# Evened code masks, a filtered sequence in other buffers, and earlier splits in a vision tower on one core

## The reference

```python
h = 2 * Re(einsum(x * (A - 1) / log A, A ** t))         # t = 0..1023: (32, 64, 1024)
h = h + attention(layernorm(h)) @ Wo                    # 16 heads of 64, rotary, causal
h = h + layernorm(h) @ (NF4_CODE[w_idx] * absmax).T + b # 4-bit codes, 1024 x 1024
h = h + mamba(layernorm(h))                             # width 2048, 16 states, gates, W_out
n = layernorm(h)
h = h + n @ W_base.T + b_base + 2 * sum over top 2 of 8 experts of w_e * (n @ A_e.T) @ B_e.T
```

## Time and profile before

| | us |
|---|---|
| median of 3 runs | 4259.92 (4257.6 to 4260.49) |
| the profiled execution's own time | 4258.99 |
| its span | 4256.8 |
| PE busy | 3949.5 (93%) |
| DVE busy | 2745.8 (65%) |
| POOL busy | 2167.9 (51%) |
| ACT busy | 2014.9 (47%) |

### The profile page before, as it was taken

How to read it: one execution, slowest core, us unless ns; L and a number is a source line. 1 busy time by engine, 2 the same in 40 slices (tenths; PEclk the granted TensorE clock), 3 DMA queues, 4 the chain that set the end, 5 groups by cost and what they waited for, 6 DMA issues and landing times.

```text
span 4256.8 us, 58578 instructions
## 1 busy us (share of the span) xinstructions
PE 3949.5 (93%) x22408; PEld 2606.4 (61%) x22408; DVE 2745.8 (65%) x3035; ACT 2014.9 (47%) x2958; POOL 2167.9 (51%) x912
## 2 busy tenths in 40 slices
PE   3779999899999999899999999999999999989998
PEld 1558777444667777544567877644377877744466
DVE  7745562899445564699725555499935556289943
ACT  5642344777332244677523234577633234477732
POOL 0023433788533333688633334488833343378852
PEclk7989999999999999999999999999999999999999
DMA  3332223000222223100123223200032222300021
GB/s 98 80 129 80 84 101 113 25 15 15 105 86 81 84 80 119 63 15 15 58 94 104 70 79 117 97 15 15 21 114 94 80 85 102 112 25 15 15 87 65
DMA packets 93813, 303.22 MB, mean 71 GB/s; under 512 B 11520, under 2 KB 15872, under 8 KB 91008
## 3 DMA queue, kind: packets, MB, share of 16 engines
q1 hardware_dynamic: 84352, 283.04, 20.1%
q10 hardware_dynamic: 9216, 16.78, 1.0%
HBM read 255.74 MB, written 44.04 MB: 70 GB/s over the span
## 4 chain that ended last, share of the span: by engine, by line
PE 51%; issue 28%; POOL 9%; DVE 9%; ACT 1%; DMA 0%; POOLq 0%; DVEq 0%; ACTq 0%
PE psg L908 20%; PE psx L1154 10%; POOL sb_wl L523 9%; PE psg L1169 8%; DVE sb_wst L1703 6%; PE psg L978 3%; PE psg L1183 2%; PE psg L983 1%; PE psg L1131 1%; PE psx L1196 1%; PE psg L1180 1%; PE psg L1141 1%; DVE psg L1676 1%; PE psg L1281 1%; DVE psg L1675 1%
## 5 line engine op out<-in xcount | busy, mean ns | idle before, releaser
L523 POOL TENSOR_TENSOR sb_wl<-sb_raw,sb_wh 128x1024 fp32r<-128x1024 f32 x388 | 960.5, 2480 | 1878.8 <-ACT sb_wh L621 1878.4
L1703 DVE TENSOR_TENSOR_SCAN sb_wst<-sb_dA,psx 128x1024 f32<-128x1024 f32 x512 | 1140.1, 2271 | 36.9 <-ACT sb_dA L751 23.7
L1154 PEld LDWEIGHTS psx<-sb_dgB,sb_duT 64*128 64x128 f32 x4096 | 358.9, 189 | 525.8 <-DVE sb_wst L1703 260.1
L751 ACT ACTIVATE sb_dA<-sb_dlt,sb_a_sb 128x504 f32<-128x504 f32 x1024 | 646.4, 705 | 61.3 <-DVE sb_wst L1703 55.7
L1154 PE MATMUL psx<-sb_dgB,sb_duT 64*128 64x256 f32 x4096 | 590.1, 408 | 86.2 <-DVE sb_wst L1703 84.5
L621 ACT ACTIVATE sb_wh<-sb_raw 128x1024 fp32r<-128x1024 f32 x388 | 407.0, 1053 | 538.2 <-PE psg L908 196.5
L556 POOL TENSOR_TENSOR sb_wst<-sb_wst,sb_cb_lo 128x1024 f32<-128x1024 f32 x256 | 599.3, 2364 | 90.0 <-DVE sb_wst L1703 90.0
L556 POOL TENSOR_TENSOR sb_wst<-sb_wst,sb_cb_hi 128x1024 f32<-128x1024 f32 x256 | 598.4, 2359 | 75.6 <-DVE sb_wst L1703 75.6
L908 PE MATMUL psg<-sb_xh,sb_wh 128*128 128x512 f32 x2080 | 539.5, 402 | 37.2 <-POOL sb_wl L523 31.7
L1169 PE MATMUL psg<-sb_wst,sb_cst 64*64 64x512 f32 x4096 | 558.8, 618 | 10.3 <-POOL sb_wst L556 9.6
L908 PE MATMUL psg<-sb_xh,sb_wl 128*128 128x512 f32 x2080 | 517.5, 391 | 0.0
(11 more groups left out here) (277 smaller groups left out, 5046.6 us busy)
## 6 DMA issues: line engine op xcount, KB each, us to landing
sb_raw<-in_w SPq DMA_DIRECT2D x360, 512.0 KB, 3.5
sb_raw<-w_ffn_dequantized SPq DMA_DIRECT2D x32, 512.0 KB, 3.2
gates<-sb_gt ACTq DMA_DIRECT2D x64, 256.0 KB, 2.4
sb_gin<-gates SPq DMA_DIRECT2D x64, 256.0 KB, 2.7
sb_dqi<-in_w_idx SPq DMA_DIRECT2D x32, 256.0 KB, 4.9
h_after_tok<-sb_h SPq DMA_DIRECT2D x4, 2048.0 KB, 8.8
sb_h<-h_after_tok SPq DMA_DIRECT2D x4, 2048.0 KB, 7.8
out<-sb_h SPq DMA_DIRECT2D x4, 2048.0 KB, 7.2
```

The lines of the kernel that those rows point to most:

```text
L523: pool.tensor_tensor(rest(b, i0), raw[:, i0 % RAW, :, :], high(b, i0).bitcast(F32), ALU.subtract).then_inc(s_wl, 1)
L751: ins_ = A(dA[:, (m * NQ + k) % RING, :, n, 1:S], dlt[:, m % 2, :].rearrange("p (b s) -> p b s", b=NB)[:, :, 1:S], ACT.Exp, scale=a_sb[:, ...
L1154: ins_ = mm(psx[:, 2 * j + r, :].rearrange("p (a t e) -> p a t e", a=8, e=2)[:, :, :, e], duT[r0:r0 + 64, m % 2, i * P:(i + 1) * P], dgB[r ...
L1703: v.tensor_tensor_scan(wst[:, x, 4 * j:4 * j + 4, :, :].rearrange("p b n s -> p (b n s)"), dA[:, x, 4 * j:4 * j + 4, :, :].rearrange("p b ...
```

## The change

1. *Masks.* ACT makes four of the eight masks in the first nine halves and three in the others (`BY_ACT`, `BY_DVE`), with rings of three and four buffers. Nine halves come before the filters and then one in each group but the last (`EARLY`, `LATE`).
2. *Conversions.* ACT converts a half one half ahead (`converted`), and issues the code loads itself, right behind the conversion; SP no longer does. On DVE the scales' product of half i - 2 comes ahead of the masks of half i, and the table's steps and the masks alternate in another order, with the first masks at the very start.
3. *Buffers.* `ah` and `al` are placed ahead of `xc`, `xh` and `xl`, so that they are what lies over the stored parts of `hT`. DVE's wait on `s_keep` moves from the first norm to the first write of `al`, ACT gets one before the first `ah` and one on `s_h0` before the first `u`. `tB` becomes another name of `tA`; `lb`, `yh`, `yl` and `dgB` move; the parameters' norm uses `sq` for `tB`.
4. *Block 0.* The load of strip 2 stands behind the first store and that of strip 3 behind the second; SP's wait for the stores moves to the end of block 0. ACT splits two strips ahead of the first norm and the third behind it.
5. *Adapters' stage.* ACT splits base strip 1 ahead of the norm, 2 and 3 behind it and 4 behind the Exp of L840.

```diff
-BY_ACT = 3
-BY_DVE = PAIRS - BY_ACT
-RING_ACT, RING_DVE = 2, 3
+RING_ACT, RING_DVE = 3, 4
-EARLY = 5
-LATE = [[5, 6], [7], [8, 9], [10], [11, 12], [13], [14], [15]]
+EARLY = 9
+LATE = [[9], [10], [11], [12], [13], [14], [15], []]
+BY_ACT = [4 if i < EARLY else 3 for i in range(HALVES)]
+BY_DVE = [PAIRS - n for n in BY_ACT]
...
# SyncE
-                if i + 2 < HALVES:
-                    sp.wait_ge(s_dqf, i + 1)
-                    load_codes(i + 2)
...
                         for n in (2, 3, 1):
                             sp.dma_start(h0[n], ...).then_inc(s_keep if n > 1 else s_h0, 16)
-                        first_strips(0, 2, 4)
-                        sp.wait_ge(s_h0, 16)
-                        sp.wait_ge(s_keep, 32)
+                            if n > 1:
+                                first_strips(0, n, n + 1)
...
# ScalarE
-            def masks(i):
+            def converted(i):
                 q = i % 2
                 act.wait_ge(s_dqi[q], i // 2 * 32 + 32)
                 if i >= 2:
-                    act.wait_ge(s_mkd, (i - 1) * BY_DVE)
+                    act.wait_ge(s_mkd, DVE0[i - 1])
                 A(dqf[:, q, :, :], dqi[:, q, :, :], ACT.Copy).then_inc(s_dqf, 1)
+                if i + 2 < HALVES:
+                    act.wait_ge(s_dqf, i + 1)
+                    load_codes(act, i + 2)
+
+            def masks(i):
+                q = i % 2
+                if i == 0:
+                    converted(0)
+                if i + 1 < HALVES:
+                    converted(i + 1)
                 act.wait_ge(s_dqf, i + 1)
...
             masks(0)
+            masks(1)
             Sin of tab[:, 0]
-            masks(1)
+            masks(2)
             Sin of tab[:, 1]
-            masks(2)
+            masks(3)
             Sin of tabs
+            masks(4)
             Sin of gco, Exp of etab, etabs and gco
-            for i in range(3, EARLY):
+            for i in range(5, EARLY):
                 masks(i)
...
-                    for i in range(AHEAD):
+                    for i in range(AHEAD if b else 2):
                         split(b, i)
                     norm(b, 0)
+                    if b == 0:
+                        split(b, 2)
...
-                    for i in range(WOUT0 + AHEAD, BASE0 + 1 if stop >= 5 else LA0):
+                    for i in range(WOUT0 + AHEAD, BASE0 + 2 if stop >= 5 else LA0):
                         split(b, i)
                 if stop >= 5:
                     norm(b, 3)
-                    split(b, BASE0 + 1)
                     split(b, BASE0 + 2)
+                    split(b, BASE0 + 3)
                     act.wait_ge(s_rex, 2 * b + 1)
                     A(rt[:, 5, 0:4], rt[:, 5, 0:4], ACT.Exp).then_inc(s_rex, 1)
+                    split(b, BASE0 + 4)
...
-                    for i in range(BASE0 + 3, NSTRIP):
+                    for i in range(BASE0 + 5, NSTRIP):
                         split(b, i)
...
# VectorE
+                if i >= 2:
+                    weights(i - 2)
                 for j in range(BY_DVE[i]):
...
-                if i >= 1:
-                    weights(i - 1)
...
                     if L == 0:
-                        v.wait_ge(s_keep, 32)
                         v.wait_ge(s_cst, 16 * 6)
```

More of the change, by code:

```diff
@@ L137 @@
 FG = 8
-EARLY = 5
-LATE = [[5, 6], [7], [8, 9], [10], [11, 12], [13], [14], [15]]
+EARLY = 9
+LATE = [[9], [10], [11], [12], [13], [14], [15], []]
+BY_ACT = [4 if i < EARLY else 3 for i in range(HALVES)]
+BY_DVE = [PAIRS - n for n in BY_ACT]
+ACT0 = [sum(BY_ACT[:i]) for i in range(HALVES + 1)]
+DVE0 = [sum(BY_DVE[:i]) for i in range(HALVES + 1)]
 def pair_parts(p):
@@ L277, in tower @@
             cb_hi = sb("cb_hi", [P, 2, NB, 4, S], F32, c)
+            dgB = sb("dgB", [P, XT, NQ, 2, 4, 32], F32, c)
             wst = sb("wst", [P, RING, NB, 4, S], F32, c)
@@ L389, in loop, with load_codes @@
             return eng.Fori(0, n)
+        def load_codes(eng, i):
+            m, q = i // 2, i % 2
+            for c in range(2):
+                eng.dma_start(dqi[64 * c:64 * c + 64, q, :, :],
+                              ins["w_idx"][m].rearrange("(r p) x -> p r x", r=2)[:, :, q * HALF:(q + 1) * HALF]).then_inc(s_dqi[q], 16)
         @block.sync
@@ L667, in _ @@
                             act.wait_ge(s_ao, b * KC + j)
+                            if b == 0 and j == 1:
+                                act.wait_ge(s_keep, 32)
                             A(ah[:, j - 1, :], ao[:, :, :].rearrange("p b s -> p (b s)"), ACT.Copy).then_inc(s_ah, 1)
@@ L763, in prm_root @@
                         own = Own(act, s_act, b * U_ACT + 3)
-                        own.link(A(tB[0:PRM, :], psx[0:PRM, 1, :], ACT.Ln, bias=C("eps_rms")[0:PRM, :]))
-                        A(tB[0:PRM, :], tB[0:PRM, :], ACT.Exp, scale=-0.5).then_inc(s_prmA, 1)
+                        own.link(A(sq[0:PRM, 1, :], psx[0:PRM, 1, :], ACT.Ln, bias=C("eps_rms")[0:PRM, :]))
+                        A(sq[0:PRM, 1, :], sq[0:PRM, 1, :], ACT.Exp, scale=-0.5).then_inc(s_prmA, 1)
                     def prm_high():
@@ L1384, in reduce_turns @@
                 own.link(ts(dst, dst, PI_IN, -PI_IN, ALU.min, ALU.max))
+            masks(0)
             own.link(tt(reg, ph.unsqueeze(2).to_broadcast([P, S, 32]),
@@ L1427, in _ @@
                 own.link(tt(tabs[:, t, :, :], tabs[:, t, :, :], etabs[:, :, :], ALU.mult))
-            masks(3)
+            masks(5)
             v.wait_ge(s_tabA, 7)
@@ L1452, in _ @@
                 own.link(stt(g2, gim, C("gmix", 4 * e + 3, 1), g2, ALU.mult, ALU.add))
-            masks(4)
+            masks(6)
             v.wait_ge(s_x, 64)
@@ L1464, in _ @@
                 own.link(tt(coef[:, e, :, :], coef[:, e, :, :], x, ALU.add))
+            masks(7)
             def powers(g):
@@ L1487, in _ @@
             powers(0)
+            masks(8)
             for g in range(S // FG):
@@ L1492, in _ @@
                     masks(i)
-            weights(HALVES - 1)
+            for i in range(HALVES - 2, HALVES):
+                weights(i)
             def newton(own, var, eps, r0, r):
```

61 lines of the change are left out of this document (31 added, 30 removed).

## The result

The changed kernel takes 4204.57 us (median of four, 4200.29 to 4209.69) against 4259.28 for the kernel before in the same series: ratio 0.9871, interval [0.9858, 0.9885]. A later series gave 4201.41 (4199.69 to 4206.49); the median of all eight is 4202.5, and I compare the experiments with that. The profiled execution has an own time of 4200.29 and a span of 4198.1, 58.7 shorter than before. The forecast was 4199.

What follows compares the result with a forecast made beforehand. TensorE, busy nine tenths of nearly every slice, was taken as the bound outside the opening. Gains of 24.4 + 14 + 22 = 60.4 us cut the span from 4256.8 to 4196.4, forecasting 4199 us; range 4181 to 4218.

Steps and rivals of the forecast that it cites:

- The case that I held likeliest: Whole kernel: gains in masks and filters, block 0's start and the adapters' stage bring 4199 us; chance 0.50.
- Part A: Code masks and filters: filters start later, near 133, but the last copy ends at 224.0; gain 24.4 us.
- the rings take both waits away: Late halves between filter groups: waits of 0.66 and 0.19 us go, a half takes 4.8 for 5.98.
- Part B: Start of block 0: DVE centres right behind the mean, PE starts its strips earlier; gain 14 us.
- 10 if the later strips come late: Start of block 0: low bound of the gain if third and fourth strip still wait long behind the stores.
- the earlier loads: Start of block 0: the last half is stored before the filters end, so strip loads go out about 1 us sooner.
- Part C: Adapters' stage, four blocks: base strips split earlier, PE's waits and low clock shrink; 5.5 us each, 22 in all.
- The hold: Adapters' stage: POOL's split of base strip 4 blocks small DVE operations, making them 2.4 us late.
- Rival 1: Adapters' stage: POOL doesn't hold the small DVE operations, this stage gains 30 us, time 4191; chance 0.20.
- Rival 2: Masks and filters: first part slower or halves don't shrink, gain there 11 to 15 us, time 4210; chance 0.17.
- Rival 3: Start of block 0: loads stay behind the stores, gain there only 8 us, time 4205; chance 0.09.
- Rival 4: Filters: TensorE stays at the lower clock, 89 us more there, 29 slower than now, 4289; chance 0.02.

Runs made afterwards that it cites:

- e5: Changed kernel with the four loads of the input sequence issued only when the first product of weights is ready: 4199.80 us.
- e9: Changed kernel with mask rings of two and three buffers, as before, in place of three and four: 4219.12 us.
- b1: Changed kernel with base strip 4 split behind the adapters' last operations, the sequence loaded later and the codes' loads issued by SP: 4188.66 us.
- b2: b1 with ACT's masks of the fifth half put behind its exponentials in place of ahead of them: 4179.31 us.
- e2: Changed kernel with the start of block 0 ordered as before, the buffers' new places kept: 4214.39 us.
- e4: Changed kernel with code masks, rings, codes' loads and filter groups as before; block 0 and adapters stay changed: 4226.79 us.
- e1: Changed kernel with the adapters' stage ordered as before the change: 4226.13 us.
- c1: The changed kernel run again, unaltered: 4201.41 us.
- e8: Changed kernel with eight halves of masks ahead of the filters, not nine, and ACT's fifth half behind its exponentials: 4194.57 us.
- e6: Changed kernel with the codes' loads issued by SP, each once its conversion is done, none by ACT: 4199.84 us.
- b5: Changed kernel with base strip 4 split behind the adapters' last operations and the input sequence loaded later: 4193.33 us.
- e3: Changed kernel with base strip 4 split behind the adapters' last operations in place of ahead of them: 4197.28 us.

## Why the prediction was right

The time was 5.6 us above the forecast at the median of the first series, 3.5 at that of all eight, well inside 4181 to 4218; the profiled execution's 4200.29 against 4198.6. The case that I held likeliest came true in its mechanism in all three parts, and its terms were off by a few us in both directions:

- **Part A, 24.4: 20.2.** The Exps ended at 85.7, not 81.2: the conversions, pairs and issues cost what was worked out (the issue pair 1.40, and 1.70 once), but two waits for loads of codes, 5.5 us, weren't in the sum; e5 shows that 4.06 of it was DMA work that could have waited. The two stops of ACT on PE before the filters made 3.27 + 1.79 = 5.1 for the 5 that I took. The filters started at 136.57 for 133. From there on the sum held: a group and a half take 11.97 for 11.9, 91.6 in all for 90.4 plus a drain. The claim that the rings take both waits away is shown by e9. Who is last was right as well: behind the exponentials ACT took 50.5 us to its last mask (50.8 in the prediction), and DVE 44.5 to its own (44.8). What the prediction didn't see is what the order costs once ACT has less to do: in b1 DVE's place behind the exponentials comes back as 15.8 us of stops, and b2 gains 10.7 by moving it. The count of seven issue pairs beside the filters should have been four; it changed nothing, since PE was the fullest engine there.
- **Part B, 14: 13.0 by e2's third strip** (from its last matmul group, 273.0 against 260.0), and 15.5 by the two traces, where the next strip starts at 261.82 for 297.56 and 20.2 of that is part A. The 6 us between mean and pair are there, 238.25 - 232.13 = 6.1, and the new wait is 2.09 for 2.2. The bound "10 if the later strips come late" wasn't needed: ACT waits 5.28 for the strip after them, at 259.96, and PE has no idle row between 256.23 and 330. What I put at 1 for the earlier loads is 3 in e4, loads and clock together, and belongs to part A's groups.
- **Part C, 22: 24.7 by e1's profile, 23.6 by its median.** Strip 3 of a block starts 4.8 earlier for 4.2, the clock gives 1.3 for 1.3; a block's period falls from 993.3 to 986.5, 6.8 for 5.5. Of the 0.7 beyond 4.8 + 1.3 another 0.4 is the clock on the strip's second group (1.98 for 2.35); the other 0.3 I haven't traced. Three times 6.8 leave 4.3 for the last block, where the clock behind the hold takes part of the gain. The hold, taken from the row of `rsin`, came as put down in the first of the operations named and with the length named.
- **Rival 1** (no hold) is refuted by the four rows of 2.37, and its price of 8 was too high: without the hold the kernel gains 5, because the prediction took a freed wait at its full length in each of the four blocks and three of them give it back. **Rival 2** had the right direction for part A and less than half of its size. **Rival 3** fell with 232.13, right behind the mean. **Rival 4** fell with the window from 136.57 to 228.19: clock 1.00. The granted clock is 0.79 from 100 to 120, where the change put work for PE, and was 0.54.

The sum 60.4 against 58.7 by the spans is closer than its terms, and that is luck: minus 4.2 in A and minus 1.0 in B stand against plus 2.7 in C. The measured terms make 57.9; the 0.8 that is left belongs to none of them.

## What to carry to other kernels

Where several engines interlock ahead of a stage, look at what the last one still waits for. ACT was busiest and last here, but its stops came from DVE's late masks, and the cheap fix was to move ACT's work from in front of a result that DVE waits for to behind it (b2, 10.7 us at the last copy for two changed lines, once the issues were off ACT). A freed wait on TensorE's path isn't worth its length by itself: the same one came to nothing over a block where the next norm gave it back, and to 4.5 us in the last block, where a second wait followed at once and the clock fell. Price what comes behind it too. Depth of a ring is worth testing by itself: without one buffer per side 12 us of the 20 in the opening are lost (e9).

## What the runs showed of the hardware

**From the third strip on, the same instructions repeat to 0.4 us, but on more than one course of the clock.** From the last matmul group of the third strip (`xl`) to the end of the span, behind its first group (`xh`, eight matmuls), the profiles need:

| kernel | third strip's xh group | from its xl group to the end |
|---|---|---|
| changed; c1; e5 | 2.11 us each | 3938.1; 3938.0; 3938.4 |
| e2 (no wait ahead of it) | 1.98 | 3938.0 |
| e8 | 3.46 | 3938.1 |
| e6; e9; e4 | 3.63; 3.66; 3.62 | 3941.1 each |
| b5; b2 (no hold) | 2.14; 2.12 | 3933.6; 3934.0 |
| b1; e3 (no hold) | 3.66; 3.68 | 3940.1; 3943.5 |

Within the first four rows the instructions from there on are the same, and so they are within the last two. In the changed kernel the third strip's first eight matmuls took 2.11 behind a wait of 2.09 (shown above at 256.23); in b1 the timeline of PE has

```profile
250.81 3.66 PE L932 MATMUL psg<-sb_xh,sb_wh 128*128 128x512 f32 x8 [2.10 <-POOL sb_wl L531]
```

The group runs at the higher level in one and largely at the lower one in the other, behind a wait of the same length. What decides it isn't shown. The start of the group differs between the kernels (253.3, 256.2 and 256.9 with 2.11; 251.0, 252.9, 269.8 and 280.1 with 3.5 to 3.7), but 252.9 and 253.3 lie close together. Nor does the group settle the rest: e8 had the low one and then the shorter course. So an opening that is 6.6 us shorter (e6) brought 2.7 at the median, and one that is 12.3 longer (e9) cost 16.6.

e3's profiled execution is 15 us above its three others. Against b5, which has the same blocks, 9.9 of that lie behind the third strip's xl group and 1.5 in its xh group, at a mean clock of 0.974 over the span in place of 0.976; 3.7 lie in the opening, against the changed kernel's. b1's, 9.7 above its median, has 6.5 and 1.5 in the same places. The Trainium skill, "TensorE: Matmul & The Clock Gate", section "Part 1: The HAM clock gate (the "warmup" mystery)", says that the chip's watch on TensorE's activity runs freely and doesn't restart with a kernel, so that the point where the clock changes varies from run to run; the traces agree that the same waits meet either outcome. I take this as the reason why the changed kernel scatters by 10 us and the kernel before by 3; a profile of a high execution of the changed kernel itself wasn't had, so that stays an inference.
